# Query products divided by halves of the pairs of blocks instead of channels, with a signal for each half

## What is computed

```python
def step(S, inp):                                   # two steps for each token
    g, a_t, b_t, k_t, v_t, q_t = inp
    bS = jnp.einsum('bhk,bhkv->bhv', b_t, S)
    S = jnp.exp(g)[..., None] * S + a_t[..., None] * bS[:, :, None, :] + k_t[..., None] * v_t[:, :, None, :]
    o = jnp.einsum('bhk,bhkv->bhv', q_t, S)
    return (S, o)
_, o = jax.lax.scan(step, S0, seq)
...
y = out * jax.nn.sigmoid(x @ Wog1 @ Wog2)           # then an RMS norm by head, @ Wo
x = _layernorm(x + attention)
x = _layernorm(x + (x @ W.T + b) + x @ lilora_weight.T)
```

## Time and profile before

| | |
|---|---|
| median of 3 runs | 2535.23 us (2530.41 to 2536.88) |
| the profiled execution | 2536.87 us, span 2535.0 us |
| busy: PE, PEld | 2121.5 us (84%), 1591.0 us (63%) |
| busy: DVE, ACT, POOL | 1764.5 us (70%), 1627.2 us (64%), 838.3 us (33%) |
| DMA | 40.4% of 16 engines, 120 GB/s mean |
| mean granted PE clock | 0.96 |

### The profile page before, as it was taken

How to read it: one execution, slowest core, us unless ns; L and a number is a source line. 1 busy time by engine, 2 the same in 40 slices (tenths; PEclk the granted TensorE clock), 3 DMA queues, 4 the chain that set the end, 5 groups by cost and what they waited for, 6 DMA issues and landing times.

```text
span 2535.0 us, 191611 instructions
## 1 busy us (share of the span) xinstructions
PE 2121.5 (84%) x85960; PEld 1591.0 (63%) x85960; DVE 1764.5 (70%) x4196; ACT 1627.2 (64%) x3048; POOL 838.3 (33%) x805
## 2 busy tenths in 40 slices
PE   6777888888888888888888888888888888889784
PEld 3556666666666666666666666666666666666573
DVE  3567567777766777766777766677876677776643
ACT  3656566666666666666666666666667666666554
POOL 1133233333333333323333323333333333332330
PEclk8889999999999999999999999999999999999886
DMA  3343244443344444344444344444334444433431
GB/s 100 85 120 113 90 132 136 139 130 98 120 130 139 133 129 121 105 123 138 137 131 131 96 124 136 131 139 128 111 117 124 137 137 132 130 98 120 131 111 38
DMA packets 558366, 305.46 MB, mean 120 GB/s; under 512 B 417186, under 2 KB 517152, under 8 KB 558240
## 3 DMA queue, kind: packets, MB, share of 16 engines
q1 hardware_dynamic: 558240, 304.19, 40.4%
HBM read 35.66 MB, written 16.78 MB: 21 GB/s over the span
## 4 chain that ended last, share of the span: by engine, by line
PE 57%; DVE 22%; issue 15%; ACT 5%; DMA 1%; SPq 0%; DVEq 0%; ACTq 0%
PE bank L582 15%; PE bank L716 8%; PE bank L741 7%; PE wide L724 7%; PE wide L732 4%; DVE uq_a L1162 4%; DVE inv L1166 4%; ACT t_t L890 3%; DVE dd L1248 3%; PE bank L655 3%; PE bank L614 2%; DVE change L1113 2%; PE bank L605 2%; PE bank L599 2%; DVE k_col L1267 2%
## 5 line engine op out<-in xcount | busy, mean ns | idle before, releaser
L475 POOL TENSOR_TENSOR state<-state,change 128x512 f32<-128x512 f32 x252 | 347.2, 1378 | 1354.2 <-DVE change L1113 1354.2
L582 PE MATMUL bank<-x_col,w_kqv 128*128 128x512 f32 x768 | 372.4, 622 | 55.9 <-issue 43.7
L741 PE MATMUL bank<-uq_now,s_now 32*32 32x24 f32 x32768 | 364.4, 187 | 9.0 <-issue 7.3
L741 PEld LDWEIGHTS bank<-uq_now,s_now 32*32 32x32 f32 x32768 | 350.4, 105 | 14.4 <-issue 10.2
L724 PE MATMUL wide<-wa_now,delta 32*32 32x80 f32 x16512 | 350.2, 234 | 3.2 <-ACT wa_now L874 2.5
L860 ACT ACTIVATE delta<-wide 128x256 f32<-128x256 f32 x256 | 98.1, 383 | 388.0 <-DVE change L1113 383.6
L1137 DVE COPY_PREDICATED aq<-ci,bank 128x128 f32<-128x128 int32 x256 | 77.3, 302 | 346.7 <-PE bank L716 218.3
L724 PEld LDWEIGHTS wide<-wa_now,delta 32*32 32x32 f32 x16512 | 308.3, 108 | 4.9 <-DMA wa_now<-aq 2.8
L479 POOL TENSOR_TENSOR state<-state,edge 128x512 f32<-128x512 f32 x252 | 292.7, 1161 | 19.8
L732 PEld LDWEIGHTS wide<-x_now,t_now 32*32 32x32 f32 x16448 | 174.0, 108 | 149.0 <-issue 148.6
L1105 DVE TENSOR_TENSOR o_col<-qs,wide 128x64 f32<-128x64 f32 x512 | 89.2, 215 | 252.2 <-PE wide L724 249.9
(11 more groups left out here) (96 smaller groups left out, 3827.4 us busy)
## 6 DMA issues: line engine op xcount, KB each, us to landing
s_now<-state SPq DMA_DIRECT2D x256, 256.0 KB
uq_now<-uqv SPq DMA_DIRECT2D x256, 192.0 KB
t_now<-t_t SPq DMA_DIRECT2D x256, 128.0 KB
uq_a<-uqv SPq DMA_DIRECT2D x64, 384.0 KB, 3.1
low<-uqv SPq DMA_DIRECT2D x64, 384.0 KB
x_col<-in_xt_dram SPq DMA_DIRECT2D x32, 512.0 KB, 3.9
w_a<-w_col SPq DMA_DIRECT2D x64, 256.0 KB, 3.7
inv<-w_col SPq DMA_DIRECT2D x64, 256.0 KB
```

The costliest lines, as they stand in the source:

```text
L475: pool.tensor_tensor(mine, mine, change[m % 2][:, :, :, :].rearrange("p m b v -> p (m b) v"), ALU.add).then_inc(s_added.handle, 1)
L582: mm = pe.matmul(ps[:, :], w_kqv[:, a, w, f * P:(f + 1) * P], x_col[:, a, :], start=a == 0, stop=a == KT - 1)
L741: mm = pe.matmul(p1_bank[quarter(h), m, b, :], s_now[quarter(h), m, b, :], uq_of(uq_now, m % HF)[quarter(h), m // HF, b * RQ:(b + 1) * RQ] ...
```

## The change

DVE makes the products in two halves of the pairs, pairs 0 to 7 and then 8 to 15 (both blocks of each). A half is two U instructions (one for each step, now over both halves of the channels) and one Q instruction. Each half raises `u_ready` and `q_ready` once, so both count 2 for a group. SP waits for the signals of half 0, issues `stage_uq(1 - c, 0)`, waits for those of half 1, and issues `stage_uq(1 - c, 1)`. DVE's wait for `drained["q"]` stands ahead of the first U. The number of instructions, their elements and the transfers are as before.

```diff
-        u_ready = signal("u_ready", 1)
+        u_ready = signal("u_ready", 2)
-        q_ready = signal("q_ready", 1)
+        q_ready = signal("q_ready", 2)
...
-                        u_made, q_made = held(sp, first, u_ready.at(j + 1, 1)), held(sp, second, q_ready.at(j + 1, 1))
-                        sp.wait_ge(u_ready.handle, u_made)
-                        sp.wait_ge(q_ready.handle, q_made)
-                        stage_uq(1 - c, 0)
-                        stage_uq(1 - c, 1)
+                        for k in range(2):
+                            u_made = held(sp, first, u_ready.at(j + 1, k + 1))
+                            q_made = held(sp, second, q_ready.at(j + 1, k + 1))
+                            sp.wait_ge(u_ready.handle, u_made)
+                            sp.wait_ge(q_ready.handle, q_made)
+                            stage_uq(1 - c, k)
...
-                    for f in range(HF):
+                    dve.wait_ge(drained["q"].handle, drained["q"].at(j + 2, HF))
+                    rows = uqv[c][:, :, 0:HF * UQ].rearrange("p q (x r) -> p x q r", r=RQ)
+                    keys = kb_col[:, :, :].rearrange("p f (b q t) -> p (f b) q t", b=GB, t=TB)
+                    asked = q_col[:, :, :].rearrange("p f (b q t) -> p (f b) q t", b=GB, t=TB)
+                    falls = ep[:, :, :, :].rearrange("p f (b q) s -> p (f b) q s", b=GB)
+                    for i in range(2):
+                        own = slice(i * TILES // HF // 2, (i + 1) * TILES // HF // 2)
                         for s in range(STEPS):
-                            last = dve.tensor_tensor(by_token(uq_of(uqv[c], f), RQ, slice(s, ROWS, STEPS)),
-                                                     tokens_of(kb_col[:, f, :]), slots_of(ep, f, s), ALU.mult)
-                    last.then_inc(u_ready.handle, 1)
-                    dve.wait_ge(drained["q"].handle, drained["q"].at(j + 2, HF))
-                    for f in range(HF):
-                        last = dve.tensor_tensor(by_token(uq_of(uqv[c], f), RQ, slice(ROWS, RQ)),
-                                                 tokens_of(q_col[:, f, :]), slots_of(ep, f, 1), ALU.mult)
-                    last.then_inc(q_ready.handle, 1)
+                            last = dve.tensor_tensor(rows[:, :, own, s:ROWS:STEPS], keys[:, :, own, :],
+                                                     falls[:, :, own, s:s + TB], ALU.mult)
+                        last.then_inc(u_ready.handle, 1)
+                        dve.tensor_tensor(rows[:, :, own, ROWS:RQ], asked[:, :, own, :],
+                                          falls[:, :, own, 1:1 + TB], ALU.mult).then_inc(q_ready.handle, 1)
```

## The result

| | before | after |
|---|---|---|
| median of 4 runs each, us | 2534.06 (2530.41 to 2536.88) | 2493.60 (2485.68 to 2497.61) |
| ratio, 95% interval | | 0.9837 (0.981 to 0.9865) |
| profiled execution, us | 2536.87, span 2535.0 | 2494.16, span 2492.3 |
| mean granted clock | 0.960 | 0.958 |

The kernel became 40 us faster, 42.7 between the two profiled executions. The lines of the code stand one lower behind the edit at L378 (scores L717, projection L583, products L1305 and L1308, mask L1138, ACT's copy L919, shift L1153).

The account below looks back on a forecast made before the run. Bound: PE's wait before score step 0 for six products, an issue and a transfer, in 29 iterations. 33.9 + 6.5 + 1.5 + 1.0 + 5.5 - 1.5 = 46.9 us off 2536.87 gives 2490; forecast 2484 to 2500, range 2476 to 2512.

Parts of the forecast that it names:

- lead-in 1.0: PE's 11.2 us wait in the lead-in ends on the same transfer; could give 0 to 2.1, taken as 1.
- first 1.5: First of PE's 29 waits before score step 0, 2.05 us long; could give 0 to 2.05, taken as 1.5.
- three short waits 2.8: Part of seven waits before score step 0, 0.89 to 0.96 us each, forecast to go whole: 6.5 us together.
- the extra waits: One more wait on DVE and two more register moves on SP, forecast to cost 1.5 us over 29 iterations.
- 33.9: Gain in us from 21 waits before step 0 (38.5 us): the smaller of wait and shift-to-step-1 distance less 1.05.
- clock 5.5: Clock falls at step 0 in 4 of the 21, 1.37 us each, forecast to go with the wait: 5.5 us.
- The path: Six DVE products, SP's issue, the transfer, score step 0; the first issue was to come about 2.1 us earlier.
- The cost of the products: DVE's products in their new form were to keep the median, 783 ns, and 0.70 us spacing.
- The slower rival: DVE's products dearer in the new form, between slot 7 and the shift: 2552 us, chance 0.05.
- the 0.67 us that the prediction put into the rule: Length of each of POOL's two L504 instructions; by the rule half 0's transfer would come some 0.6 us later.
- The gate behind the shift: Score step 1 can start no sooner than 1.05 us behind the end of DVE's layer norm shift.
- signs of being wrong: First transfer late, products above 0.8 us, PE's wait reappearing before step 1 or 3, clock falling as often elsewhere.

Follow-up runs that it names:

- experiment 1: The changed kernel with SP waiting for both halves' signals ahead of the first U and Q transfer: 2538.48 us, ratio to before 1.0012.
- Experiment 6: The changed kernel with products divided by blocks, the second block's three moved to the next slot behind the statistics: 2497.57 us, ratio to before 0.9825.
- experiment 4: The changed kernel with PE's first four transposes of slot 7 run twice: 2499.64 us, ratio to before 0.9849.
- its second profile: The changed kernel run again without any edit: 2494.24 us, ratio to before 0.9823.
- the third experiment: The kernel before with one extra 512-element DVE product ahead of its six: 2563.25 us, ratio to before 1.0097.
- the seventh experiment: The changed kernel with products divided by blocks and PE's first four slot 7 transposes run twice: 2496.1 us, ratio to before 0.9824.

## Why the prediction was right, and where its sizes were off

The kernel measures 2493.60 us where the forecast was 2490, with 2484 to 2500 around it, and by the path that it described. The sum of 46.9 us against 42.7 between the profiled executions:

| stretch | forecast | measured |
|---|---|---|
| up to the sixth step 0 (lead-in 1.0, first 1.5, three short waits 2.8, less 0.2 of the extra waits) | 5.1 | 5.2 |
| 25 iterations (33.9 + four short waits 3.7 + clock 5.5 - 1.3 of the extra waits) | 41.8 | 36.1 |
| the end | - | 1.4 |

The forecast for the 25 is 5.7 us too high. From the products' start to step 1 it is 7.0 too high; 1.3 came in elsewhere in the iterations. With the 1.4 of the end, these are 2.7 us for which the prediction had no term, so it is partly luck that the total is nearer than its parts.

**The path: right, shown.** The first issue is 2.06 us ahead of the second, and experiment 1 puts the whole gain on it.

**The cost of the products: right.** The rows that answer, the changed kernel's two lines of products (count, ns min/median/max):

```profile
L1305 DVE TENSOR_TENSOR uqv<-kb_col,ep x128: 677/757/1533, 39.6 to 2310.2; 128x512 f32<-128x512 f32 x128
L1308 DVE TENSOR_TENSOR uqv<-q_col,ep x64: 676/783/792, 40.8 to 2310.8; 128x512 f32<-128x512 f32 x64
```

The median stays at 0.76 to 0.78. The slower rival had nothing to stand on, and the 1.5 us for extra waits can't be seen: experiment 1, which has them too, stands at 1.0012 with an interval that takes in 1. As to the rule of the Trainium skill's SBUF — State Buffer, section Who interferes with whom, that as the prediction priced it would have kept half 0 behind two POOL instructions: these do run beside half 0,

```profile
1425.09 1.94 DVE L1305 TENSOR_TENSOR uqv<-kb_col,ep 128x512 f32<-128x512 f32 x2
1426.95 0.79 DVE L1308 TENSOR_TENSOR uqv<-q_col,ep 128x512 f32<-128x512 f32 x1
...
1425.86 1.34 POOL L505 TENSOR_TENSOR edge<-ep,em 128x32 f32<-128x32 f32 x2
```

and half 0 is done 2.65 us behind its start, with the second product and Q starting 0.70 apart as in the earlier trace rows. So the sum was right to go by the rows. But the 0.67 us that the prediction put into the rule is not POOL's work alone, and so the rows don't refute the rule. Experiment 6, where half of the products stand elsewhere, has both without the other (count, ns min/median/max):

```profile
L512 POOL TENSOR_TENSOR edge<-tail,em x62: 264/495/728, 87.8 to 2315.3; 128x32 f32<-128x32 f32 x62
L1183 DVE TENSOR_TENSOR uqv<-q_col,ep x64: 680/687/790, 39.6 to 2327.2; 128x512 f32<-128x512 f32 x64
```

A POOL instruction of this size takes 0.26 to 0.28 us where no such product runs and 0.72 beside one; a product takes 0.66 to 0.69 where POOL is idle and 0.75 to 0.79 beside these. So they do hold each other up, but POOL bears most of it and DVE some 0.1 us a product; the spacing of 0.70 contains that, where products alone start 0.58 to 0.60 apart. Whether the one is locked out for the other's whole instruction these rows don't tell.

**The gate behind the shift: right, the size 1.23 and not 1.05.** The prediction took 0.06 + 0.99 from the earlier trace rows; what it left out is the step from the last copy to PE's start. By its own rule (the smaller of the wait and the distance less the gate) 1.23 makes 31.2 us of the 21 waits, not 33.9. The rule had also taken the wait whole in the four iterations with a fall at step 0, though 1.37 of their distance is the fall itself, which the sum counts a second time as the clock's: 1.1 us too much. In the changed kernel the ten iterations that hang on the gate lie at 10.09 to 10.17 us from the products' start to step 1, 10.12 on the mean. The forecast needed 11.77 - 41.8 / 25 = 10.10 as the mean of all 25, four iterations with a fall in slot 7 among them. With those four at 10.65, as such iterations measure, and the other 21 at the gate the 25 sum to 2.6 us more than the forecast. That is what the gate's size cost.

**The 21 long waits: the mis-sized step.** The prediction let PE come to step 0 in the new kernel as it came in the old, each in its own iteration. The 15 iterations that don't reach the gate take 10.55 on the mean. Ten have a fall in slot 7 and 10.65 us, six more than before had: 6 by 0.53 are 3.2 us. In five the transfer is late, and they take 10.36: 5 by 0.24 are 1.2. With the gate's 2.6 these make the 7.0. Neither of the two had a term in the sum.

*PE itself, in ten.* These start step 0 at 7.01 to 7.12 behind the products' start, because the clock has fallen in slot 7. The transposes of `tt` and the window around them, in the iteration ahead of 476.07 (columns as above), beside the iteration of 548.67, where it didn't fall:

```profile
467.83 2.07 PE L707 MATMUL bank<-cf,both 128*128 128x128 f32 x12 [0.73 <-DVE x_row L1288]
...
465.00:467.00 2.00, 1.08 (x50) 0.81 (x36) 2.00 (x7) 0.00 (x0) 0.00 (x0) 1.00 0.16 45
467.00:469.00 2.00, 1.27 (x10) 1.18 (x10) 1.97 (x6) 0.38 (x1) 1.64 (x2) 0.91 0.75 240
469.00:471.00 2.00, 2.00 (x81) 1.67 (x83) 2.00 (x4) 1.90 (x5) 1.92 (x3) 0.50 0.97 219
...
541.46 1.53 PE L707 MATMUL bank<-cf,both 128*128 128x128 f32 x12 [0.73 <-DVE x_row L1288]
```

PE was busy 1.08 and 1.27 of two microseconds each, then the granted clock is 0.50 (1.2 GHz) while it is fully busy, and the scan behind takes longer. The same falls explain the prediction's short waits: in the kernel before, the last four of them, at 2056.82, 2131.64, 2206.51 and 2281.22, have L706 ahead of them at 2.82, 2.80, 2.52 and 2.17. There a fall was hidden: PE came late to a transfer that came later still. Of 25 iterations before has 4 such falls, experiment 1 has 6, the changed kernel 10 and its second profile 9. So as the wait went, falls that it had covered came to light, and more of them came. One costs 0.5 us at step 1, as the gate takes the rest. Why there are more of them isn't settled; experiment 4, which fills the gap ahead of the transposes, has none.

*The transfer, in five.* The prediction had it land within 3.29 us, "alone it should take no more", and DMA idle where it was put. That is one iteration. In five others W is issued only 2.6 to 2.7 us ahead of it, where the kernel before never had less than 4.6 in its 25:

```profile
1499.11 0.63 SPq L362 DMA_DIRECT2D w_a<-w_col  x1
1499.89 0.62 SPq L362 DMA_DIRECT2D inv<-w_col  x1
1501.73 0.59 SPq L357 DMA_DIRECT2D uq_a<-uqv  x1
...
DMA to landing us min/median/max: 4.0/4.0/4.0
...
1502.00:1503.00 1.00, 1.00 (x115) 0.97 (x101) 1.00 (x3) 1.00 (x3) 0.87 (x2) 1.00 0.83 186
...
1505.77 1.56 PE L717 MATMUL bank<-uq_a,w_a 32*32 32x48 f32 x128 [0.23 <-issue]
```

DMA is 0.83 busy in the first microsecond of this transfer, where the earlier trace rows shows 0.00, and it takes 4.0 us instead of 3.0. The five land at 3.7 to 4.0 us, and their iterations take 10.2 to 10.6. How far ahead W is doesn't order it alone: with 3.0 us the transfer lands in 2.9 again, with 4.2 in 3.3 to 3.4. What is shown is that the earlier place is not empty in all iterations; the prediction looked at one. That W delays the transfer isn't shown by a run of its own.

W itself is late wherever the clock has fallen in a third place: in slot 5, in the matmuls L606, some 23 us ahead of step 0. The iteration of 1505.77, and that of 476.07, where it didn't fall there:

```profile
1483.37 3.11 PE L606 MATMUL bank<-ss_col,cf 128*128 128x512 f32 x4
...
452.98 1.88 PE L606 MATMUL bank<-ss_col,cf 128*128 128x512 f32 x4
```

The changed kernel has nine such iterations, and the five late transfers are all among them. In the nine, slot 7's transposes start 0.9 to 1.0 us ahead of the products instead of 2.5 to 2.6, and SP issues the first W transfer between 0.4 us ahead of the products' start and 0.1 behind it, instead of 1.5 to 2.0 ahead. The kernel before has eight of them; there `uqv` left 2 us later and landed in 3.0 to 3.1 all the same.

**The clock: right at step 0, not in sum.** The prediction took 5.5 us for the four falls at step 0 as going with the wait. They did go: the changed kernel has none there. But in the 25 iterations the clock falls 19 times instead of 16: in slot 5 nine times (before: eight), in slot 7 ten times (before: four), at step 0 never (before: four). So it does fall as often in another place, which the prediction had named as a sign of being wrong, and the 3.2 us of slot 7 take back more than half of the 5.5.

**What would show it.** PE's issue wait is 18.5 us (forecast 11 to 15); step 1 waits a little, 0.28 to 0.46 us in six of the ten iterations at the gate and under 0.1 in the others; products at 0.70; iterations 73.5 us (forecast some 73). Of the signs of being wrong two came true in part: the first transfer lands late in five of 25, and the clock falls in another place.

## What to carry to other kernels

When a consumer waits for the first of several transfers, divide the producer's work by what that transfer carries, not by what is convenient to compute, and let it go on its own signal: the work was the same, and 1.6% of the time went. Before you count such a wait as gained, list in each iteration what comes next behind it (here three things: a gate at 10.12 us, PE's own lateness, and a late transfer), since the wait hides them and its length says nothing of them. And price a slow stretch of the clock by what it does to the next meeting point: falls in slot 7 that cost 1 us on PE cost 0.5 on the path, and the work put in to prevent them cost elsewhere what it saved. Count the falls in the whole iteration, too: W left late in each of the nine iterations in which the clock had fallen some 23 us earlier.

## What was not expected of the hardware

A wait of 2.26 to 2.65 us brought a half-clock stretch in 14 of 18 iterations, waits of 1.65 to 2.05 in 4 of 21 before the change and in none of the first experiment, so the third experiment's 0.75 us of DVE work cost up to 36.5 us in one profiled execution, and its times spread over 22.7 us (2550.74 to 2573.41) where the changed kernel's spread over 12. The mean granted clock is no guide to the time: 0.960 before, 0.958 after, and 0.969 in the fourth experiment, which is not faster than the changed kernel. The 384 KB transfer of `uqv` took 3.0 to 3.2 us from issue to landing in each of before's 25 iterations; in the changed kernel it took 2.9 to 3.0 in 13, 3.3 to 3.4 in seven and 3.7 to 4.0 in five, and up to 4.1 in the seventh experiment. And a small POOL instruction beside DVE's products takes 0.72 us where alone it takes 0.27, so its length in a row is no price of its work.
